# A mixer's TensorE stream in another order: x rows, inner product and turned tiles regrouped

## The reference

```
x = x + 0.5 * ffn(layernorm(x))
x = x + mixer(layernorm(x))
x = x + 0.5 * ffn(layernorm(x))
```

```
gate, xBC, dt = split(h @ in_proj_w.T)
x, B, C = split(silu(causal_conv4(xBC) + conv_b))
dt = softplus(dt + dt_bias); A = -exp(A_log); x = x * dt
Y_diag = ((C B^T) * exp(segsum(A dt))) x        # within a chunk
states = (B * decay_to_end)^T x, carried from chunk to chunk
Y_off  = (C states) * exp(cumsum(A dt))         # from the carried states
y = (Y_diag + Y_off + D * x) * silu(gate)
out = rmsnorm(y) * norm_w @ out_proj_w.T
```

## Time and profile before

| what | value |
|---|---|
| runs | 1648.75, 1644.76, 1648.19 us; median 1648.19 |
| the profiled execution | 1646.44 us; its span 1644.6 us |
| granted TensorE clock, mean | 0.999 |
| busy: PE, PE weight load | 1619.7 us (98%), 1312.1 us (80%) |
| busy: DVE, ACT, POOL | 1035.5 (63%), 626.1 (38%), 379.1 us (23%) |
| HBM | 176 GB/s over the span |

### The profile page before, as it was taken

One profiled execution on the slowest core, in us unless ns is written; L12 is line 12 of the kernel. 1 busy time (PEld: TensorE's weight loads), 2 busy tenths in 40 slices (PEclk: granted clock), 3 DMA queues, 4 the chain that ended last, 5 costly groups with the idle time before them and its releaser, 6 DMA issues.

```text
span 1644.6 us, 25044 instructions
## 1 busy us (share of the span) xinstructions
PE 1619.7 (98%) x9672; PEld 1312.1 (80%) x9672; DVE 1035.5 (63%) x2022; ACT 626.1 (38%) x934; POOL 379.1 (23%) x298
## 2 busy tenths in 40 slices
PE   6999999999999999999999999999999999999999
PEld 3788888877888778888877888877888878888887
DVE  6544445776677877777776777777775684543333
ACT  4333434463333463333464334265333341122111
POOL 1656663011221212122122122122122121000000
PEclk9999999999999999999999999999999999999999
DMA  9746564754544444454445445445444447566763
GB/s 291 298 148 245 203 222 166 268 183 143 170 156 151 154 162 145 156 168 151 150 146 167 158 148 173 157 129 195 156 156 157 156 126 223 167 181 192 214 203 129
DMA packets 253427, 290.46 MB, mean 177 GB/s; under 512 B 14464, under 2 KB 211200, under 8 KB 244096
## 3 DMA queue, kind: packets, MB, share of 16 engines
q1 hardware_dynamic: 253312, 288.88, 53.8%
HBM read 238.51 MB, written 50.33 MB: 176 GB/s over the span
## 4 chain that ended last, share of the span: by engine, by line
PE 74%; DVE 2%; ACT 1%; issue 1%; DMA 0%; SPq 0%; ACTq 0%; DVEq 0%
PE bank L1190 31%; PE bank L1231 14%; PE bank L1146 12%; PE bank L1259 5%; PE bank L1328 3%; PE bank L1299 2%; PE bank L1315 2%; PE bank L1277 2%; PE bank L1287 1%; PE bank L1322 1%; DVE xT L1749 0%; PE bank L1174 0%; DVE res L1775 0%; PE bank L1156 0%; DMA cum_stay<-m_aS 0%
## 5 line engine op out<-in xcount | busy, mean ns | idle before, releaser
L1190 PE MATMUL bank<-fxT,wj 128*128 128x512 f32 x1752 | 415.2, 390 | 0.0
L1190 PEld LDWEIGHTS bank<-fxT,wj 128*128 128x128 f32 x1752 | 328.6, 188 | 68.6
L1231 PE MATMUL bank<-m_wd,m_hb 128*128 128x512 f32 x1128 | 278.8, 392 | 0.0
L1231 PEld LDWEIGHTS bank<-m_wd,m_hb 128*128 128x128 f32 x1128 | 209.2, 188 | 44.8 <-issue 2.4
L1543 ACT CAST m_hb<-xn 128x512 fp32r<-128x512 f32 x96 | 59.5, 620 | 452.6 <-DVE xn L1762 452.6
L1146 PE MATMUL bank<-xT,wi 128*128 128x512 f32 x900 | 222.9, 395 | 1.6 <-DVE m_cv L1791 0.5
L1146 PEld LDWEIGHTS bank<-xT,wi 128*128 128x128 f32 x900 | 166.1, 188 | 39.6 <-issue 5.1
L1775 DVE TENSOR_TENSOR res<-bank,res 128x512 f32<-128x512 f32 x192 | 132.5, 690 | 83.0 <-PE bank L1231 80.9
L2098 POOL TENSOR_TENSOR m_L<-m_L,m_GT 128x512 f32<-128x512 f32 x36 | 52.7, 1464 | 431.9 <-ACT m_L L1552 431.9
L1762 DVE SCALAR_TENSOR_TENSOR xn<-bank,sc,xn 128x512 f32<-128x512 f32 x96 | 71.8, 747 | 121.7 <-PE bank L1190 121.6
L1537 ACT ACTIVATE xn<-bank,sc 128x512 f32<-128x512 f32 x96 | 66.1, 688 | 146.4 <-PE bank L1190 140.9
(11 more groups left out here) (224 smaller groups left out, 2319.2 us busy)
## 6 DMA issues: line engine op xcount, KB each, us to landing
wj<-ug_split SPq DMA_DIRECT2D x167, 512.0 KB, 4.2
m_wd<-dn_split SPq DMA_DIRECT2D x48, 1024.0 KB, 4.8
wi<-in_split SPq DMA_DIRECT2D x76, 512.0 KB, 3.3
ug_split<-b_wu SPq DMA_DIRECT2D x8, 2048.0 KB, 14.3
m_wo<-out_split SPq DMA_DIRECT2D x32, 512.0 KB, 4.1
wi<-ug_split SPq DMA_DIRECT2D x25, 512.0 KB, 4.2
in_split<-b_msp SPq DMA_DIRECT2D x20, 512.0 KB, 4.0
raw<-in_wug SPq DMA_DIRECT2D x8, 1024.0 KB, 7.0
```

The lines of the kernel that those rows point to most:

```text
L1190: ins = pe.matmul(to[:], w[:, a, k, :], frm[:, b, k, :], start=(k == 0 and i == 0), stop=(k == KH - 1 and i == 2))
L1231: ins = pe.matmul(F[t % 2][:], hb[:, a, j, ck(t)], wd[:, b, j, :], start=(j == 0 and n == 0), stop=(j == 1 and n == 2))
```

## The change

Three things are put in another order; no instruction is added or taken away.

- PE, in every block but the first of all (`at` = 0) and the last of an item: `ydiag` comes right behind `times_start` (before, behind `gate1`), and `x_rows` of the next block comes right behind `from_states` (before, at the head of the next block). Each of 27 blocks is concerned.
- ACT, in the same blocks: `silu(at, 1)` and `x_silu(q, b + 1)` come right behind the exponent `times`, ahead of `hidden_high(at, 0)` and `square`.
- PE, between items (three times): the turns 0 and 1 stand together ahead of `down` 0, the turns 2 and 3 ahead of `down` 2.

```diff
@@ tensor, the blocks
-                    x_rows(q, b)
+                    if b == 0 or at == 1:
+                        x_rows(q, b)
                     decay(q, b, 0)
...
                     times_start(q, b)
+                    if at and not end:
+                        ydiag(q, b)
                     if b:
                         up0(at)
...
                     if at == 0:
                         gate0(at + 1, 0)
-                    ydiag(q, b)
+                    if at == 0 or end:
+                        ydiag(q, b)
                     from_states(q, b)
+                    if at and not end:
+                        x_rows(q, b + 1)
                     if not end:
                         in_proj(q, 6 + 2 * b)
@@ tensor, between items
                 beside_turn(q + 1, 0)
+                beside_turn(q + 1, 1)
                 down(at, 0, NPAIR * (q + 1) - 1)
-                beside_turn(q + 1, 1)
                 down(at, 1)
                 beside_turn(q + 1, 2)
+                beside_turn(q + 1, 3)
                 down(at, 2)
-                beside_turn(q + 1, 3)
                 down(at, 3)
@@ scalar, the blocks
                     times(q, b)
+                    if at and not end:
+                        silu(at, 1)
+                        x_silu(q, b + 1)
                     if at:
                         hidden_high(at, 0)
...
-                    if at:
+                    if at == 0:
+                        x_silu(q, b + 1)
+                    elif end:
                         silu(at, 1)
                     if not end:
-                        x_silu(q, b + 1)
                         gate(q, b + 1)
```

## The result

| | before | with the change |
|---|---|---|
| median of the runs | 1648.75 us (5 runs, 1644.76 to 1650.55) | 1659.85 us (5 runs, 1656.67 to 1660.22) |
| profiled execution, its span | 1646.44, 1644.6 us | 1659.85, 1657.9 us |

The ratio is 1.0071, with a 95% interval of 1.0058 to 1.0083: slower by 11.1 us of the medians, 13.3 us of the spans. The forecast was 1657.0, within 1649.7 to 1663.0, at 0.72 for slower.

A forecast was written before the change was run, and what follows sets the result against it. PE, busy 98% of the span, was taken to bound the kernel. Terms 1.9 + 4.1 + 1.9 + 0.6 + 1.8 - 0.2 = +10.1 us on 1646.44 or 1648.19 gave 1657, range 1649.7 to 1663.

The forecast's parts named there:

- Seams of the regrouping: In 27 blocks, x_rows and ydiag in new places: +0.07 us a block, +1.9 us, bounds -4.9 and +7.0.
- at least 0.35, I take 0.48: x_rows behind from_states: 0.48 us, about 0.13 of it a seam between plain forms; 0.46 at the block's head.
- ydiag's +0.05: ydiag behind times_start loses its seam with from_states, adds an exit and an entry into up0: +0.05 us a block.
- under 1.9 us from from_states to in_proj: Sign of a wrong forecast, in ordinary blocks: from_states to in_proj takes less than 1.9 us.
- The wait at x_rows: Blocks 4 and 6, seven: PE waits for conv plus x_silu, 0.59 us new each, +4.1 us; F is from_states' start.
- hidden_high behind x_silu: hidden_high about 1.05 us later delays hidden: block 1 of items 1 to 3 +1.9 us, block 2 +0.6 us.
- cheap seams: Rival: seams at their cheap end, -4.9 us in place of +1.9, 1649.7, no change; chance 0.17.
- Block 7 gets nothing: x_rows leaves its head, but its second decay waits longer for the first exponent: 4 x 0.46 = +1.8 us.
- Turns in pairs: Between items, two groups of four transposes become one: about -0.03 us each, 6 of them, -0.2 us.
- Every block waits: Rival: the slack at x_rows and the head is gone, 0.25 us more in each of 27 blocks, 1663.5; chance 0.15.
- Conv is not late: Rival: in blocks 4 and 6 conv ends before F + 0.9, x_rows doesn't wait, 1641; chance 0.08.

The follow-up runs named there:

- the root cut: DVE's layer norm root cut two Newton steps earlier: on the changed kernel 1653.04 us, ratio 1.0031; on the kernel before 1644.51 us, ratio 0.9981.

## Why the prediction was right, and where not

The direction, the main cause (PE waiting behind conv and x_silu in seven blocks) and the size came out as forecast. That the forecast lay within 3 us of the median owes something to luck: terms that were 2.5 us too high and 4.7 us too low stood against each other.

- **Seams of the regrouping:** +0.07 a block was predicted, -0.02 to -0.03 measured, in 27 blocks 2.5 us less than the +1.9. The mis-sized term is x_rows, "at least 0.35, I take 0.48": moved with ACT's order it measured 0.36, next to its lower bound. The seam between two plain forms that I took from ydiag and from_states hardly occurs here. ydiag's +0.05 was +0.02 to +0.03 by itself. The sign "under 1.9 us from from_states to in_proj" came for this reason (1.87).
- **The wait at x_rows, seven blocks:** +0.59 predicted, +0.60 to +0.65 measured (the seams' -0.03 within it); the cause is shown by the root cut (no wait). The waits were 0.7 each, not 0.8 to 0.9, since conv ended 0.15 earlier against F. The working used 0.42 for the moved x_rows here and in block 1, where the seams took 0.48, and gave no reason; with 0.48 these two terms would have been 0.4 and 0.2 us lower.
- **hidden_high behind x_silu:** right for block 1: hidden_high at F + 1.30, a wait of 0.63 three times (0.8 had been said), +2.2 for +1.9. Hidden comes 0.99 later in place of 1.05, PE 0.25 in place of 0.42. For block 2 it was mis-sized: 0.2 predicted, 0.40 to 0.43 measured, at the first `down` of the next block. The step set 1.05 of delay against 1.0 of room, and still took 0.2. In block 2.2 hidden_low ends 0.93 later against F (963.33 for F = 952.85, before 953.89 for 944.34), but PE would be at that `down` 0.20 earlier (decay at F + 10.13 and 0.22 behind it, before F + 10.23 and 0.32), and starts 0.26 behind hidden_low's end (963.59): the first of these hangs on the cheap seams, and the second was left out. What the step did not say is that the whole loss needs both edits: ydiag away from gate1 and ACT's new order.
- **Block 7 gets nothing:** right. The second decay waits 0.56 in place of 0.20, first to second decay 4.25 for 3.90, in all four.
- **Turns in pairs, -0.2:** here a term was missing. "DVE and ACT have the tiles in time; if not, each loses at most a few tenths" looked at the tiles, not at the sums, whose round trip through DRAM ends at the next item's first decay. The turns grew by 2.9 us in this trace, 2.3 of it in waits for the sums, and block 2.0 by 1.6 more in clock. How much of this the pairs make is not shown. They take 0.45 us of room from the trip (7.66 for 8.11), but alone they cost nothing that can be told; with single turns 1.4 of the 2.3 remain; x_rows moved with single turns and ydiag as before shows 0.6 there, and ydiag alone 1.1.
- **The sum:** +10.1 on a span that rose 13.3; the medians rose 11.1. Seams 2.5 too high, the waits of blocks 4, 6, 1 and 3 together 1.7 too low, block 7 0.4 too high, turns and the clock behind one of them 4.7 too low; the other fall of the clock (1.6, block 0.0) and the shorter start (1.7) cancel.
- **Rivals.** The cheap seams came true in part: -0.03 a block, between the +0.07 taken and the -0.18 of that rival. "Every block waits" is out: no wait on x_silu at L1287 in any but the seven. (Its 1663.5 is a slip; 1656.5 + 6.8 is 1663.3.) "Conv is not late" did not come by itself, but the root cut made it so, and then the kernel is still slower (1.0031), by blocks 1, 3, 5 and 7 and the turns.

## What to carry to other kernels

A short group on the bound engine can be the cover under which a second engine finishes something for a third: before moving it, list what starts at the group's beginning and must be done at its end, and price edits that share such a chain together, since here two that cost nothing apart cost 5.6 us in one. Count an engine's slack at each kind of block, since the ordinary blocks, the most by number, had none of the 13 us and gave back 0.3. Where a step can be made to wait for late work (conv behind a root), move the late work first: that one line alone made the kernel 0.2% faster, and made a sevenfold wait of the change vanish.

## What the runs showed of the hardware that I had not expected

The granted clock can fall around waits of half a microsecond, and does so in some traces only. In block 0.0 PE stands 0.65 us at from_states and 0.54 at the projection behind it. In the changed kernel:

```profile
371.69 4.58 PE L1146 MATMUL bank<-xT,wi 128*128 128x512 f32 x12 [0.54 <-DVE m_cv L1801]
```

```profile
371.00:373.00 2.00, 1.46 (x5) 1.07 (x5) 1.73 (x3) 0.63 (x1) 0.19 (x1) 0.70 0.01 4
373.00:376.00 3.00, 3.00 (x10) 2.38 (x9) 0.00 (x0) 0.00 (x0) 2.48 (x3) 0.63 0.00 0
```

In the kernel before, with the same two waits:

```profile
373.39 3.00 PE L1146 MATMUL bank<-xT,wi 128*128 128x512 f32 x12 [0.54 <-DVE m_cv L1791]
```

```profile
373.00:375.00 2.00, 1.61 (x7) 1.38 (x8) 1.44 (x3) 0.63 (x1) 0.48 (x1) 1.00 0.01 4
```

Twelve matmuls take 1.6 us more or not, by the same order of work. That projection takes the 1.6 us longer in four of the thirteen traces of this case. So one profiled execution may carry 1.6 us of chance at such a place. It shows in the times too: of the five runs of the change the two with a mean clock of 0.999 took 1657.48 and 1656.67 us, the three with 0.996 to 0.998 took 1659.85 to 1660.22. (That the spans differ by 13.3 and the medians by 11.1 has another reason: the profiled execution of before lies 2.3 below its median, that of the change is its median.) The Trainium skill ("TensorE: Matmul & The Clock Gate", Part 1: The HAM clock gate) says that the clock has two states only. The rows agree: the stretch at 877 us stands at 0.50 and none is below; the 0.70 and 0.63 above are means over a change of level.

The other was the seam: four plain transposes behind from_states cost 0.36 us, where the same four between fp32r groups cost 0.46.
